# The next pair's h behind xw_lo and the gravity exponentials, not among the t tiles

## The chip, the cores and the metric

The kernel runs on one core of a Trainium2 chip. The metric is the device time of one execution in microseconds; the kernel before was run three times. A separate execution was taken by the hardware profiler. The core's engines are TensorE (PE in the rows: matmul; PEld: its weight loads), VectorE (DVE), ScalarE (ACT), GpSimd (POOL) and SyncE (SP), whose queue issues all the transfers of the main loop.

## The reference

Two graph layers, each followed by a residual add and a layer norm, over x of shape (32, 256, 512). `adj` has shape (256, 256), and the same matrix is the weight of the first layer and the mask of the second.

```python
# layer 1
q = einsum('c,bcn->bn', wq, x); k = einsum('c,bcn->bn', wk, x)
scores = leaky(q[:, None, :] + k[:, :, None])
att = softmax(scores, -1)
out = relu(adj @ (x @ att^T) + bm)
x = layernorm(x + out)                      # this is h, called so below
# layer 2
z_l, z_g, v = h @ W_lang^T, h @ W_grav^T, h @ W_V^T
A_l = relu(cosine(z_l, z_l)) * not_eye
A_g = exp(-|z_g - z_g'|^2 / (2 sigma^2)) * not_eye
K = w_l * rownorm(A_l * adj) + (1 - w_l) * rownorm(A_g * adj)
x = layernorm(h + (K @ v) @ W_O^T)
```

## The kernel before

The 32 batches are done as 16 pairs. Each engine has its own instruction stream, written out by hand, and the streams meet in semaphores; there is no planner. A pipeline of steps p = -2 to 15 works on three pairs at once: in step p the second layer of pair p, the attention and the norm that gives h of pair q = p + 1 (the flag `l0`, true up to p = 14), and the first product of pair r = p + 2 (`new`, up to p = 13). A step in the middle takes some 61 us, and the rows below are mostly of one such step, from 480 to 541 us.

Fp32 accuracy is had from fp16 products of parts: each value is split in a hi part (a cast on ScalarE) and a lo part (value minus hi, on VectorE or GpSimd), and a product is three matmuls, hi by hi, lo by hi, hi by lo. In the profile these are L254, L255 and L256 for every product.

The order of a main step on TensorE is: z products of pair p (L254 to L256 with `ul`, `ug`), attention products of pair q, transposes of the aggregate, the four t products (`t_product`: k = 0, 1 language, k = 2, 3 gravity; two batches each), three xw products of pair r, the adding of transposes (`add_transposed`, L446) and the rows of norms (L261 with `r_l`), the other xw products in between, three v products, the transposes of K (`turn_k`, L478: four for each batch, which wait for `k_done`), `k_rows`, the last v product and the o products.

What the other engines do around the change, in the order of the streams:

- VectorE: `sq_tile` (L1054), `sq_bound` (L1062), `h_tile` (L968: h = (y - mean) * rstd, a tensor_scalar from SBUF to SBUF, 512 columns), `t_lo_tile` (L1069), `neg_g_tile` (L1077), `xw_lo_tile` (L909, L910), `masked_rows`, `a_l_tiles` (L1110), `a_g_tile` (L1093), `q_tops`, then `degrees` (L1117 to L1129, seven instructions on four columns, each waiting for the one before; the last makes `s_l`), `v_lo_tile(0)` (L1048), and `k_tiles` (L1138: K = a_g * s_g + a_l, four instructions of 256 columns, with both tensors in SBUF). Behind these, `kt_lo`, `t_rows`, and the residual adds (L1153).
- ScalarE: `t_hi_tile` (L666, L671), `h_hi_tile` (L700: the cast of an h tile to fp16, into a part of the buffer `att_hi`), `xw_hi_tile` (L616), `exp_tile` (L677), `v_hi_tile` (L683), `k_scale` (L689: a_l times s_l, which waits for `sl_done` and releases the four `k_tiles` one by one).
- GpSimd: `r_l` (L1317), and then `h_lo_tile` (L1274: h minus h_hi, four instructions of 512 columns), each waiting for its h_hi and all of them for the last `t_lo` (`t_lo_done`, 4 p + 4). Elsewhere in the step att_lo (L1291), x_lo (L1297) and two of the four adds of y and x_res (L1305; VectorE does the other two, L946).
- SyncE's queue, in order: `turn_h` (a DMA transpose of h_hi, L215, when all four h_hi are done, and one of h_lo, L218), then the copy of x to `x_res` and the load of the next x. The z products of the next step wait for both transposes (`ht_hi_landed`, `ht_lo_landed`).

In the trace h_hi and h_lo bear the names att_hi and att_lo, v_hi and v_lo the names z_hi and z_lo, the transposed K the names t_hi and t_lo.

Of the kernel before, what the change touches and what calls it, by code (L numbers as in the profile page):

```python
# [51 lines left out]
def build(nc, x, adj, adjT, wqk, bm, wl, wg, wv, woT, gate, sigma, out):  # L52
# [10 lines left out]
    with ExitStack() as ctx:  # L63
# [98 lines left out]
        def h_of(pair):  # L162

            return h2[:, pair % 2]
# [381 lines left out]
        def _(act):  # L546
# [66 lines left out]
            def xw_hi_tile(p, k):  # L613
                r = p + 2
                act.wait_ge(s["wx_mm"], 8 * r + k + 1)
                act.activation(xw_hi[:, k // NC, k % NC, 0:O], wx_bank(p, k)[:, 0:O], ACT.Copy)\  # L616
                   .then_inc(s["xw_hi_done"], 1)
# [30 lines left out]
            def step(p, l0, new):  # L648
                if p < 0:
                    return early(p)  # L650
                q, r = p + 1, p + 2
# [5 lines left out]
                def t_hi_tile(k):  # L657
                    act.wait_ge(s["t_mm"], 4 * p + k + 1)
                    if k < 2:
                        source = halves[4 + k]  # L660
                    else:

                        j = k - 2
                        act.wait_ge(s["neg_g_done"], 2 * p + j + 1)
                        for c in range(OC):
                            last = act.activation(a_g[:, j, c, :], halves[4 + k][:, c, :], ACT.Identity,  # L666
                                                  bias=neg_g[:, 2 * j + c:2 * j + c + 1])
                        last.then_inc(s["shift_done"], 1)
                        act.wait_ge(s["shift_done"], 2 * p + j + 1)
                        source = a_g[:, j]  # L670
                    act.activation(t_hi[:, k], source, ACT.Copy, scale=2.0 ** -6).then_inc(s["t_hi_done"], 1)  # L671

                def exp_tile(j):
                    act.wait_ge(s["s_mm"], 4 * p + 3 + j)
                    act.wait_ge(s["neg_gs_done"], 2 * p + j + 1)
                    for c in range(OC):
                        last = act.activation(halves[6 + j][:, c, :], halves[6 + j][:, c, :], ACT.Exp,  # L677
                                              bias=neg_gs[:, 2 * j + c:2 * j + c + 1], scale=c_grav[:, 0:1])
                    last.then_inc(s["exp_done"], 1)

                def v_hi_tile(k):
                    act.wait_ge(s["v_mm"], 4 * p + k + 1)
                    act.activation(v_hi[:, k, :], bank[v_bank[k]][:], ACT.Copy).then_inc(s["v_hi_done"], 1)  # L683
# [14 lines left out]
                def h_hi_tile(k):  # L698
                    act.wait_ge(s["h_done"], 4 * q + k + 1)
                    act.activation(h_hi[:, k, :], h_of(q)[:, k, :], ACT.Copy).then_inc(s["h_hi_done"], 1)  # L700
# [22 lines left out]
                        z_hi_tile(g)  # L723
                t_hi_tile(0)
                t_hi_tile(1)
                if l0:
                    h_hi_tile(0)
                    h_hi_tile(1)
                t_hi_tile(2)
                if l0:  # L730
                    h_hi_tile(2)
                    h_hi_tile(3)
                t_hi_tile(3)
                if new:
                    for k in range(3):
# [7 lines left out]
                if new:  # L743
                    for k in range(6, 8):
                        xw_hi_tile(p, k)
                exp_tile(1)
                if new:
                    v_hi_tile(0)
                k_scale()
# [17 lines left out]
        def _(dve):  # L767
# [123 lines left out]
            def o_norm(pair, j):  # L891
                if j == 0:
                    dve.wait_ge(s["o_rstd_done"], pair + 1)
                    dve.wait_ge(s["o_mv_done"], pair + 1)
                for k in (2 * j, 2 * j + 1):
                    last = dve.tensor_scalar(o[:, k, :], o[:, k, :], o_mv[:, k, 0:1], o_rstd[:, k:k + 1],  # L896
                                             ALU.subtract, ALU.mult)
                last.then_inc(s["normed"], 1)

            def den(q, k):  # L900
                dve.wait_ge(s["ot_mm"], 8 * q + k + 1)
                wait(dve, s["agg_done"], 8 * (q - 1) + k + 1)
                dve.reciprocal(den_inv[:, k:k + 1], bank[k % 4][:, O:O + 1])\  # L903
                   .then_inc(s["den_done"], 1)
# [8 lines left out]
            def q_tops(r):  # L913
                dve.wait_ge(s["xw_lo_done"], 8 * r + 8)
                dve.tensor_reduce(q_part[:], q_cols, AX.X, ALU.max).then_inc(s["q_part_done"], 1)
# [17 lines left out]
            def att_tile(q, g):  # L933

                j, n = g // NC, g % NC
                dve.wait_ge(s["vb_done"], 8 * q + g + 1)
                wait(dve, s["att_lo_done"], 8 * q + g - 1)
                dve.scalar_tensor_tensor(out=att[:, g % 2, :], in0=a_row[:, j, :], scalar=u_col[:, j, n:n + 1],  # L938
                                         in1=vb_of(q, g), op0=ALU.mult, op1=ALU.max)\
                   .then_inc(s["att_done"], 1)  # L940
# [23 lines left out]
            def h_tile(q, k):  # L964
                if k == 0:
                    dve.wait_ge(s["y_rstd_done"], q + 1)
                    dve.wait_ge(s["y_mv_done"], q + 1)
                dve.tensor_scalar(h_of(q)[:, k, :], y[:, k, :], y_mv[:, k, 0:1], y_rstd[:, k:k + 1],  # L968
                                  ALU.subtract, ALU.mult).then_inc(s["h_done"], 1)
# [66 lines left out]
            def step(p, l0, new):  # L1036
                if p < 0:
                    return early(p)
                q, r = p + 1, p + 2

                def z_lo_tile(g):
                    dve.wait_ge(s["z_hi_done"], 8 * p + g + 1)
                    dve.tensor_tensor(z_lo[:, g, :], bank[g % 4][:], z_hi[:, g, :], ALU.subtract)\  # L1043
                       .then_inc(s["z_lo_done"], 1)
# [44 lines left out]
                def a_g_tile(j):  # L1089
                    dve.wait_ge(s["exp_done"], 2 * p + j + 1)  # L1090
                    for c in range(OC):
                        k = 2 * j + c
                        last = dve.scalar_tensor_tensor(out=a_g[:, j, c, :], in0=halves[6 + j][:, c, :], scalar=1.0,  # L1093
                                                        in1=mask[:, c, :], op0=ALU.min, op1=ALU.mult,
                                                        accum_out=deg_g[:, k:k + 1])
                    last.then_inc(s["ag_done"], 1)
# [60 lines left out]
                def o_stats():  # L1157
                    if p > 0:
                        for k in range(4):
                            o_stat_tile(p - 1, k)  # L1160
                        o_mean(p - 1)

                def o_norms():
                    if p > 0:
                        o_norm(p - 1, 0)
                        o_norm(p - 1, 1)

                if l0:
                    for g in range(8):
                        att_tile(q, g)  # L1170
                        for i, after in enumerate((0, 1, 3, 4, 5, 6, 7)):
                            if g == after:
                                z_lo_tile(i)
                    z_lo_tile(7)
                    den(q, 0)
                    o_stats()
                    for k in range(1, 6):
                        den(q, k)
                    if p > 0:
                        o_norm(p - 1, 0)  # L1180
                    den(q, 6)
                    if p > 0:
                        o_norm(p - 1, 1)
                    den(q, 7)
                    for k in (0, 2):
                        y_add_tile(q, k)
                        y_stat_tile(q, k)
                    y_stat_tile(q, 1)
                    y_stat_tile(q, 3)
                    y_mean(q)  # L1190
                    sq_tile(0)
                    t_lo_tile(0)
                    sq_tile(1)
                    sq_bound()
                    h_tile(q, 0)
                    h_tile(q, 1)
                    t_lo_tile(1)
                    neg_g_tile(0)
                    h_tile(q, 2)
                    h_tile(q, 3)  # L1200
                else:
                    for g in range(8):
                        z_lo_tile(g)
                    o_stats()
                    sq_tile(0)
                    o_norms()
                    t_lo_tile(0)
                    neg_g_tile(0)
                    sq_tile(1)
                    sq_bound()  # L1210
                    t_lo_tile(1)
# [18 lines left out]
                if new:  # L1230
                    xw_lo_tile(p, 6)
                    xw_lo_tile(p, 7)
                    q_tops(r)
                a_g_tile(1)
                degrees()
                v_lo_tile(0)
# [122 lines left out]
```

## Time and profile before

| what | us |
| --- | --- |
| median of three runs | 1048.47 (1047.57 to 1049.12) |
| the profiled execution's own time | 1045.15 |
| its span, first to last instruction | 1043.4 |
| TensorE busy | 1014.2 |
| VectorE busy | 792.3 |
| ScalarE busy | 654.6 |
| GpSimd busy | 385.6 |

Mean granted clock of TensorE: 0.996 of full speed. Busy times are sums over stages that have different limits, and matmuls are pipelined, so they say which engine is full and not what a stage waits for.

### The profile page before, as it was taken

The numbers are of one execution on the slowest core, as the hardware profiler recorded it, in microseconds if no ns is written. First come the engines' busy times: TensorE is split into PE (matmuls) and PEld (weight loads), VectorE is DVE, ScalarE is ACT, GpSimd is POOL, SyncE is SP. The second block draws the span as 40 slices with busy tenths as digits, with TensorE's granted clock in tenths as the row PEclk, the third lists the DMA queues.
The fourth block names the chain that finished last, engine by engine and source line by source line (L and its number), as shares of the span: only waits on it lengthen the run. The fifth ranks groups of instructions, "written<-read, shape, count | busy, mean of one in ns | idle before, by whom it ended". The sixth has DMA issues, their size and how long they took to land.

```text
span 1043.4 us, 19673 instructions
## 1 busy us (share of the span) xinstructions
PE 1014.2 (97%) x7189; PEld 695.5 (67%) x7189; DVE 792.3 (76%) x2318; ACT 654.6 (63%) x1267; POOL 385.6 (37%) x340
## 2 busy tenths in 40 slices
PE   7888999999999999999999999999999999999995
PEld 4465848577584857758485775848577584857662
DVE  5775776878787687878768787876878787787756
ACT  2658576665857666585766658576665857666432
POOL 0335334262533426253242625324262532424200
PEclk9999999999999999999999999999999999999998
DMA  7020221314022141402214140221414022131211
GB/s 271 32 82 1 32 91 52 112 41 107 16 75 88 48 116 41 114 10 72 91 47 117 41 113 10 71 92 46 118 41 106 18 69 94 44 79 41 41 41 41
DMA packets 85233, 72.05 MB, mean 69 GB/s; under 512 B 64144, under 2 KB 64656, under 8 KB 83088
## 3 DMA queue, kind: packets, MB, share of 16 engines
q1 hardware_dynamic: 85136, 70.79, 23.4%
q8 instruction: 57, 0.93, 0.4%
q14 instruction: 40, 0.33, 0.1%
HBM read 21.50 MB, written 16.78 MB: 37 GB/s over the span
## 4 chain that ended last, share of the span: by engine, by line
PE 84%; issue 5%; DVE 1%; ACT 1%; POOL 1%; POOLq 0%; DVEq 0%; ACTq 0%
PE bank L254 25%; PE bank L255 25%; PE bank L256 25%; PE bank L338 3%; PE bank L446 2%; PE bank L261 2%; PE bank L478 1%; POOL att_lo L1274 0%; DVE o L896 0%; ACT bank L578 0%; DVE t_lo L1069 0%; ACT t_hi L671 0%; ACT a_g L666 0%; ACT z_hi L655 0%; POOLq L63 0%
## 5 line engine op out<-in xcount | busy, mean ns | idle before, releaser
L1291 POOL TENSOR_TENSOR att_lo<-att,att_hi 128x512 f16<-128x512 f32 x128 | 148.2, 1158 | 337.4 <-ACT att_hi L584 337.4
L254 PE MATMUL bank<-xw_hi,att_hi 128*128 128x257 f16 x512 | 140.4, 274 | 1.2 <-DVE wvo_lo L858 1.0
L255 PE MATMUL bank<-ht_lo,z_hi 128*128 128x256 f16 x512 | 139.6, 273 | 0.0
L254 PE MATMUL bank<-ht_hi,z_hi 128*128 128x256 f16 x512 | 139.6, 273 | 0.0
L256 PE MATMUL bank<-ht_hi,z_lo 128*128 128x256 f16 x512 | 139.6, 273 | 0.0
L256 PE MATMUL bank<-xw_hi,att_lo 128*128 128x257 f16 x512 | 139.5, 272 | 0.0
L255 PE MATMUL bank<-xw_lo,att_hi 128*128 128x257 f16 x512 | 139.1, 272 | 0.0
L1043 DVE TENSOR_TENSOR z_lo<-bank,z_hi 128x512 f16<-128x512 f32 x128 | 88.2, 689 | 48.1 <-ACT z_hi L655 48.1
L603 ACT ACTIVATE agg_t<-bank,den_inv 128x256 f32<-128x256 f32 x128 | 58.4, 472 | 79.3 <-DVE den_inv L903 78.9
L1274 POOL TENSOR_TENSOR att_lo<-h,att_hi 128x512 f16<-128x512 f32 x60 | 67.6, 1159 | 102.3 <-DVE t_lo L1069 102.3
L683 ACT ACTIVATE z_hi<-bank 128x512 f16<-128x512 f32 x64 | 37.6, 591 | 95.6 <-PE bank L256 95.6
L254 PE MATMUL bank<-wvo_hi,ht_hi 128*128 128x512 f16 x256 | 97.0, 379 | 0.0
L255 PE MATMUL bank<-wvo_lo,ht_hi 128*128 128x512 f16 x256 | 97.0, 379 | 0.0
L256 PE MATMUL bank<-wvo_hi,ht_lo 128*128 128x512 f16 x256 | 97.0, 379 | 0.0
L938 DVE SCALAR_TENSOR_TENSOR att<-a_row,u_col,bank 128x512 f32<-128x512 f32 x120 | 88.7, 739 | 9.8 <-POOL att_lo L1291 7.2
L584 ACT ACTIVATE att_hi<-att 128x512 f16<-128x512 f32 x128 | 80.2, 626 | 23.0 <-DVE att L938 23.0
L655 ACT ACTIVATE z_hi<-bank 128x512 f16<-128x512 f32 x128 | 75.0, 586 | 22.5 <-PE bank L256 22.5
L578 ACT ACTIVATE bank<-b_row,v_col 128x512 f32<-128x512 f32 x120 | 80.7, 680 | 1.2
L1305 POOL TENSOR_TENSOR y<-y,x_res 128x512 f32<-128x512 f32 x32 | 47.0, 1468 | 87.8 <-ACT y L610 87.7
L254 PE MATMUL bank<-wm_hi,x_hi 128*128 128x258 f16 x256 | 70.3, 275 | 4.1 <-DVE x_lo L981 2.5
L256 PE MATMUL bank<-wm_hi,x_lo 128*128 128x258 f16 x256 | 69.8, 273 | 0.0
L255 PE MATMUL bank<-wm_lo,x_hi 128*128 128x258 f16 x256 | 69.8, 273 | 0.0
(177 smaller groups left out, 2629.3 us busy)
## 6 DMA issues: line engine op xcount, KB each, us to landing
x_in<-in_x SPq DMA_DIRECT2D x16, 1024.0 KB, 5.5
x_res<-x_in SPq DMA_DIRECT2D x16, 1024.0 KB, 5.1
out_y<-o SPq DMA_DIRECT2D x32, 512.0 KB, 2.8
agg_t<-in_wl SPq DMA_DIRECT2D x4, 256.0 KB, 3.5
y<-in_wg SPq DMA_DIRECT2D x1, 1024.0 KB, 9.3
o<-in_wv SPq DMA_DIRECT2D x1, 1024.0 KB, 11.5
h<-in_woT SPq DMA_DIRECT2D x1, 1024.0 KB, 13.6
att<-in_adjT SPq DMA_DIRECT2D x1, 256.0 KB, 4.0
```

Source lines behind the costliest of these rows:

```text
L254: pe.matmul(dst, ah, bh, start=(i == 0 and first), stop=False, skip_group_check=skip)
L255: pe.matmul(dst, ah, bl, start=False, stop=False, skip_group_check=skip)
L256: last = pe.matmul(dst, al, bh, start=False, stop=(i == n - 1), skip_group_check=skip)
L578: act.activation(vb_of(q, g), b_row[:, j, :], ACT.Copy, scale=v_col[:, j, n:n + 1])\
L584: act.activation(att_hi[:, g // NC, g % NC, :], att[:, g % 2, :], ACT.Copy)\
L603: act.activation(agg_t[:, k // NC, k % NC, :], bank[k % 4][:, 0:O], ACT.Copy, scale=den_inv[:, k:k + 1]).then_inc(s["agg_done"], 1)
L655: act.activation(z_hi[:, g, :], bank[g % 4][:], ACT.Copy).then_inc(s["z_hi_done"], 1)
L938: dve.scalar_tensor_tensor(out=att[:, g % 2, :], in0=a_row[:, j, :], scalar=u_col[:, j, n:n + 1], in1=vb_of(q, g), op0=ALU.mult, op1=ALU.max)\
L1043: dve.tensor_tensor(z_lo[:, g, :], bank[g % 4][:], z_hi[:, g, :], ALU.subtract)\
L1274: pool.tensor_tensor(h_lo[:, k, :], h_of(q)[:, k, :], h_hi[:, k, :], ALU.subtract)\
L1291: pool.tensor_tensor(att_lo[:, n[0], n[1], :], att[:, g % 2, :], att_hi[:, n[0], n[1], :], ALU.subtract).then_inc(s["att_lo_done"], 1)
L1305: pool.tensor_tensor(y[:, k, :], y[:, k, :], x_res[:, k // 2, k % 2, :], ALU.add)\
```

## The change

The four h tiles of the next pair are computed on VectorE behind the last two `xw_lo` tiles and `q_tops`, in front of `a_g_tile(1)`, and no longer two and two between the t_lo tiles. Their casts h_hi on ScalarE stand behind `exp_tile(1)`, in front of `v_hi_tile(0)` and `k_scale`, and no longer around `t_hi_tile(2)`. In step 14, which has no pair r, the h tiles stand directly behind `a_g_tile(0)`, and the casts in front of `k_scale`. GpSimd's and SyncE's streams are not touched.

```diff
@@ scalar, step @@
                 t_hi_tile(0)
                 t_hi_tile(1)
-                if l0:
-                    h_hi_tile(0)
-                    h_hi_tile(1)
                 t_hi_tile(2)
-                if l0:
-                    h_hi_tile(2)
-                    h_hi_tile(3)
                 t_hi_tile(3)
...
                 exp_tile(1)
+                if l0:
+                    for k in range(4):
+                        h_hi_tile(k)
                 if new:
                     v_hi_tile(0)
                 k_scale()
@@ vector, step @@
                     t_lo_tile(0)
                     sq_tile(1)
                     sq_bound()
-                    h_tile(q, 0)
-                    h_tile(q, 1)
                     t_lo_tile(1)
                     neg_g_tile(0)
-                    h_tile(q, 2)
-                    h_tile(q, 3)
...
                     xw_lo_tile(p, 6)
                     xw_lo_tile(p, 7)
                     q_tops(r)
+                if l0:
+                    for k in range(4):
+                        h_tile(q, k)
                 a_g_tile(1)
                 degrees()
                 v_lo_tile(0)
```

## Rows read from the trace of the kernel before

**Rows 1.** The page, busy us (share of the span), instructions.

```profile
PE 1014.2 (97%) x7189; PEld 695.5 (67%) x7189; DVE 792.3 (76%) x2318; ACT 654.6 (63%) x1267; POOL 385.6 (37%) x340
```

**Rows 2.** Busy times in a stretch: engines, granted clock, DMA share, GB/s.

```profile
480.00:541.00 61.00, 61.00 (x445) 42.31 (x443) 47.71 (x142) 40.54 (x78) 24.55 (x21) 1.00 0.24 70
```

**Rows 3.** Waits of TensorE: for whom, us in total, times, longest.

```profile
PE bank L254 <- DVE z_lo L1043: 5.1, 3, 2.6
```

**Rows 4.** Timeline of VectorE in the middle step: start, us, instruction.

```profile
480.28 1.00 DVE L968 TENSOR_SCALAR h<-y,y_mv,y_rstd 128x512 f32<-128x512 f32 x2
...
484.21 0.29 DVE L1077 SCALAR_TENSOR_TENSOR vb<-bank,ident 128x128 f32<-128x128 f32 x1 [0.99 <-PE bank L256]
...
494.00 0.41 DVE L1093 SCALAR_TENSOR_TENSOR a_g<-bank,mask 128x256 f32<-128x256 f32 x1
...
495.36 0.22 DVE L1129 SCALAR_TENSOR_TENSOR s_l<-deg_l,c_wl,r_l 128x4 f32<-128x4 f32 x1
...
496.23 1.67 DVE L1138 SCALAR_TENSOR_TENSOR a_l<-a_g,s_g,a_l 128x256 f32<-128x256 f32 x4
```

**Rows 5.** Timeline of ScalarE in the middle step.

```profile
480.86 1.15 ACT L700 ACTIVATE att_hi<-h 128x512 f16<-128x512 f32 x2 [1.29 <-DVE h L968]
...
494.33 0.60 ACT L683 ACTIVATE z_hi<-bank 128x512 f16<-128x512 f32 x1 [1.59 <-PE bank L256]
```

**Rows 6.** Timeline of TensorE in the middle step.

```profile
499.31 1.04 PE L478 MATMUL bank<-ident,a_l 128*128 128x128 f32 x8
```

**Rows 7.** Timelines of VectorE, TensorE and GpSimd in step 14.

```profile
978.66 0.39 DVE L1117 TENSOR_TENSOR deg_l<-deg_l,r_l 128x4 f32<-128x4 f32 x1
...
980.39 1.67 DVE L1138 SCALAR_TENSOR_TENSOR a_l<-a_g,s_g,a_l 128x256 f32<-128x256 f32 x4
...
982.61 0.38 PE L254 MATMUL bank<-wvo_hi,ht_hi 128*128 128x512 f16 x1
...
974.53 4.50 POOL L1274 TENSOR_TENSOR att_lo<-h,att_hi 128x512 f16<-128x512 f32 x4 [5.43 <-DVE t_lo L1069]
```

**Rows 8.** Timeline of GpSimd in the middle step.

```profile
488.58 4.51 POOL L1274 TENSOR_TENSOR att_lo<-h,att_hi 128x512 f16<-128x512 f32 x4 [6.89 <-DVE t_lo L1069]
```

**Rows 9.** att tiles: start-up timelines, and the line's forms (ns min/median/max).

```profile
37.87 2.29 POOL L1291 TENSOR_TENSOR att_lo<-att,att_hi 128x512 f16<-128x512 f32 x2 [1.38 <-ACT att_hi L584]
...
39.14 1.57 DVE L938 SCALAR_TENSOR_TENSOR att<-a_row,u_col,vb 128x512 f32<-128x512 f32 x1 [1.34 <-POOL att_lo L1291]
...
L938 DVE SCALAR_TENSOR_TENSOR att<-a_row,u_col,bank x120: 735/739/749, 84.1 to 947.6; 128x512 f32<-128x512 f32 x120
L938 DVE SCALAR_TENSOR_TENSOR att<-a_row,u_col,vb x8: 740/746/1567, 30.6 to 45.5; 128x512 f32<-128x512 f32 x8
```

**Rows 10.** The adds of y and x_res on both engines, ns min/median/max.

```profile
L946 DVE TENSOR_TENSOR y<-y,x_res x32: 691/928/1193, 64.4 to 962.1; 128x512 f32<-128x512 f32 x32
...
L1305 POOL TENSOR_TENSOR y<-y,x_res x32: 1267/1468/1674, 65.1 to 962.7; 128x512 f32<-128x512 f32 x32
```

**Rows 11.** The lines of r_l and of the degree product.

```profile
L1317 POOL TENSOR_TENSOR r_l<-sq_lc,exponent x16: 1006/1232/1234, 114.7 to 1012.8; 128x4 f32<-128x4 f32 x16
...
L1117 DVE TENSOR_TENSOR deg_l<-deg_l,r_l x16: 156/156/390, 128.9 to 1021.0; 128x4 f32<-128x4 f32 x16
```

**Rows 12.** Busy times in stretches of the start-up, columns as in rows 2.

```profile
33.50:36.50 3.00, 0.62 (x2) 0.00 (x0) 2.33 (x8) 2.38 (x6) 1.15 (x1) 1.00 0.00 0
...
37.40:40.80 3.40, 3.40 (x8) 2.08 (x7) 2.06 (x3) 2.20 (x5) 2.29 (x2) 0.50 0.00 0
83.00:86.00 3.00, 0.43 (x3) 0.03 (x2) 1.52 (x3) 2.92 (x7) 0.14 (x1) 1.00 0.00 0
```

**Rows 13.** SP's and TensorE's timelines, and transfers (us to landing).

```profile
493.12 1.93 SPq L218 DMA_TRANSPOSE ht_lo<-att_lo  x1
...
509.04 0.38 PE L254 MATMUL bank<-ht_hi,ul_hi 128*128 128x512 f16 x1
...
ht_lo<-att_lo SPq DMA_TRANSPOSE x15, 4.4
```

## The prediction

> **What bounds the kernel now.** I read the page first. TensorE is busy for 97% of the span [rows 1]. Then the stretches: over 61 us in the middle TensorE is busy for all 61.00 us at full clock, while VectorE has 13 us to spare, ScalarE 20 and GpSimd 36 [rows 2]. TensorE's own waits name z_lo three times, the longest 2.6 us, one of them at 83 us, in the first main step [rows 3, 12]. After some 90 us, until the last product, I find no start-to-start gap on TensorE over 0.45 us. So the reader is to see this: for 14 of the 15 steps that prepare a next pair, TensorE is the bound and waits for nothing. Work that other engines do is free as long as it stays inside its slack, and nothing that they save can come back in the time. The question is only which slack this change uses up.
>
> The step of 480 to 541 us stands for the others; its time is 60.9 us.
>
> **The change part by part.**
>
> *What is removed.* Four h tiles leave the place among t_lo: two pairs of 1.00 us each, at a pitch of 0.46 us (0.54 + 0.46), 1.84 us in all [rows 4]. Behind the second pair VectorE waits 0.99 us for TensorE's next t product, and ScalarE's t_hi of that product needs what VectorE then makes of it, so all behind it comes when it came before. Of the first pair, t_lo of tile 1 comes 0.9 us earlier, but TensorE asks for it only behind the last t product and three xw products, and is busy throughout [rows 2]. Gain: nothing. On ScalarE four casts leave, a pair in 1.15 us, the first of it 0.61 [rows 5]. Nothing again.
>
> *What h now stands in front of.* Behind the last xw_lo, from 494.00, VectorE runs a_g of tile 1, the degrees, s_l, and, after ScalarE's scaling, the four K tiles, which TensorE transposes. This is one chain: s_l ends at 495.58, K tiles run from 496.23 to 497.90 [rows 4]. TensorE starts the eight transposes at 499.31, at a pitch of 0.11, so the second half of them at 499.75 [rows 6]. In the last such step the K tiles end at 982.06, and the product behind the transposes starts at 982.61, so their second half at 982.61 - 0.44 = 982.17: the hand-over takes 0.11 us [rows 7]. Slack of the chain: 499.75 - 497.90 - 0.11 = 1.74 us. The four h tiles push it by 1.84 us. By displacement alone each of 14 steps loses 0.1 us: the cover is all but spent before anything else is counted.
>
> *h_hi and h_lo.* ScalarE has been idle since 492.74 (1.59 us before v_hi) [rows 5], so h_hi of tile 0 starts when h is there: h 494.00 to 494.54, cast 494.62 to 495.23. GpSimd's h_lo waits for h_hi alone now, since the last t_lo is long done; it starts some 0.15 us after, at 495.38. Before, the four h_lo ran from 488.58 to 493.09, all of them over VectorE work that reads PSUM [rows 8]. Now four h_lo of 1.16 us at a pitch of 1.12 us lie from 495.38 on, over h tile 3, the degrees and the K tiles, and these read two operands from SBUF.
>
> *What such an overlap costs.* Four places show it. In the start-up, GpSimd's att_lo runs from 37.87 for 2.29 us, to 40.16; an att tile whose operands all lie in SBUF starts at 39.14 and takes 1.57 us, where its kind has a median of 0.746: it ends 0.54 us after GpSimd does, as if it had only then begun [rows 9]. The y adds on VectorE, two SBUF operands of 512 columns, take 0.69 us at the least, where GpSimd is idle, and 1.19 at the most, beside GpSimd's y tiles [rows 10]. The tiny degree product of four columns takes up to 0.390 us where the median is 0.156, and that is the one of the last such step, where it ends with the last h_lo (979.05 and 979.03) [rows 7, 11]. And r_l on GpSimd has a median of 1.232 us, with two h tiles (tensor_scalars from SBUF to SBUF) beside it from 480.28 to 481.28, and a least of 1.006, that of the last step, which has no h tiles [rows 4, 11]: a tensor_scalar on SBUF holds GpSimd up as well. Where all but one input is in PSUM, nothing is seen: a hundred and twenty att tiles lie between 735 and 749 ns, whether att_lo runs or not [rows 9]. So VectorE's two-SBUF-operand work waits until the running GpSimd instruction ends, however short it is itself.
>
> *The sum of it.* At the y adds the waiting VectorE instruction goes in between GpSimd's two, which follow each other directly: the first of those takes 1.27 us and the second 1.67, the 0.4 to 0.5 more being what the add holds [rows 10]. I take that for the rule: they alternate. From 495.4 on VectorE's contending instructions are h tile 3, the degree product, the two clamps, s_g, s_l and four K tiles, each a dependent small step, so nearly each meets a fresh h_lo, and VectorE is free only when the fourth has ended. That is 495.38 + 4.51 (as the four take now) = 499.89, and 0.5 us later where h tile 3 holds GpSimd back: about 500.5. By then the degrees stand at the second or third of their clamps; 0.4 us remain to the end of s_l, 500.9. From the end of s_l to the second K release it takes 497.90 - 495.58 = 2.32 us: 503.2, plus 0.11: TensorE goes on at 503.3 instead of 499.75, **3.6 us** late. TensorE has nothing else queued ahead of these transposes, and is in order, so all of it is lost. Times 14: 50.4 us.
>
> *Bounds of this term.* Below: no exclusion at all, 0.1 us a step. Between: if the four-column tensor_scalars don't contend (no row shows them beside GpSimd), only the degree product, s_l and the K tiles do; then s_l ends near 498.4, the K tiles alternate with the last two h_lo and end near 502.1, 2.5 us a step. Above: h tile 3 loses the place and the back-to-back h_lo let nobody in: they end at 499.97, then h (0.5), a_g and degrees (1.6), 502.0, plus 2.32: 4.7 us a step. I take 3.6, since the y adds show alternation and r_l under the h tiles shows that a tensor_scalar contends.
>
> On this last point the Trainium skill has a rule (SBUF — State Buffer, Who interferes with whom): a VectorE instruction with two SBUF inputs, and also a tensor_scalar in its two-port mode, and a GpSimd instruction that reads SBUF shut each other out for the whole of one instruction. By it the small clamps wait too and the step loses 3.6 us; by the rows of two-operand instructions alone it would be 2.5 us, and the total some 17 us less with the last step. The trace agrees where it has both (1.57 us for 0.746), and no row has four columns of tensor_scalar beside GpSimd.
>
> *The last such step.* It has no xw work, and the second half of the transposes starts right behind the K tiles, at 982.17 for 982.06 [rows 7]. With no slack the whole delay, 503.2 - 497.9 = 5.3 us, is lost. Once: 5.3 us.
>
> *The clock.* Twice before the steady part TensorE stands still for nearly 3 us. At 33.5 the next stretch is granted 0.50 for 3.4 us, that is 1.2 GHz instead of 2.4, after 0.62 us of work in 3.00; the stall at 83.0, with 0.43 in 3.00, came and went at full clock [rows 12]. One fall in two. A stall of 3.6 us per step is of that kind. A fall costs half of 3.4, 1.7 us. I count 6 in the 15, somewhat under one in two since there is dense work on both sides: 10.2 us (bounds: none, and all 15, 25.5).
>
> *What is behind it, hidden.* SP's queue: the hi transpose can go at 496.9, the lo transpose at 500.5 instead of 493.12. Its landing takes 4.4 us: 504.9, and the products of the next pair start at 509.04 + 3.6 = 512.6 [rows 13]. 7.7 us remain. The x_res copy and the x_in load behind them in the queue slip by the same 7 us; their readers (x_hi, the y adds) stand in the next step behind all eight z tiles, more than 7 us further on. v_hi on ScalarE behind h_hi slips from 494.33 to 496.8, and its v_lo stands just in front of the K tiles, whose turn comes at 501.5. Residuals of pair p read h of pair p, the other buffer. All free.
>
> Sum: 50.4 + 5.3 + 10.2 = 65.9 us on the profiled span of 1043.4, so 1109.3; that execution took 1045.15 (1.75 around the span), and the median of the runs shown is 3.3 above it. **1048.5 + 65.9 = 1114 us.**
>
> **The rivals.** (1) *The displacement alone.* If h_lo and the degrees don't get into each other's way, 14 x 0.1 + 1.84 + 0 = 3.2 us: 1051.7. For it speaks that busy shares leave room; against it the four places above. (2) *Not slower.* The same, with the four h tiles costing 1.74 us or less, the slack: then 14 steps lose nothing and the last loses under 1.84 us, 1050.3 or less, within 0.2% (2.1 us, about what a measurement tells). It decides at 1.74 us of total delay of s_l. Against: the pitch of 0.46 us leaves 1.84. Nothing makes it faster: TensorE has no gap to close but the 0.3 us of the last step. (3) *Partial exclusion.* The small steps slip through between h_lo's, and only one or two of them and the K tiles wait: 1 to 2.5 us a step, with little clock loss, 1065 to 1085. For it: VectorE, once waiting, goes first. (4) *No alternation and a cold clock.* 14 x 4.7 + 6.4 in the last step + 15 falls of 1.7: 98 us, 1146. For it: GpSimd's four follow at a pitch shorter than their length, which two y adds don't.
>
> **How the numbers follow.** Forecast with alternation (2.5 to 4.4 us a step, up to 10 falls): 0.65, that is 1086 to 1134. Rival 3: 0.16. Rival 4: 0.06. Rival 1: 0.06. Rival 2: 0.05. An unforeseen gain: 0.02. Range: 1066 leaves out rivals 1, 2 and the gain (0.13), 1134 leaves out 0.06. Slower: 0.65 + 0.16 + 0.06 + 0.06 = 0.93; same 0.05; faster 0.02.
>
> **What would show it.** In the changed profile: h_lo beginning some 0.15 us behind the first h_hi and lying over the degrees; degree instructions, four columns wide, that take up to 1.1 us; r_l back at 1.0 us; TensorE waiting 3 to 4 us for VectorE's K tiles in front of the transposes in every step, 5 in the last; the granted clock below 1 in several stretches behind such waits. It is wrong if the degree instructions keep 0.16 us beside h_lo, if h_lo begins after the K tiles, or if the alternation gives VectorE most of the turns, when the wait is 1 to 2 us.

## The result and the profile after

| | us |
| --- | --- |
| median before, beside this one | 1048.02 (1045.34 to 1049.12, 4 runs) |
| median after | 1108.13 (1107.30 to 1110.47, 4 runs) |
| ratio | 1.0581, 95% interval 1.0554 to 1.0608 |
| profiled span after | 1107.2, against 1043.4 |

The change costs 60 us, 5.8%. The same instructions run; of the span's 63.8 us more, TensorE's busy time takes 26.6 (1040.8 for 1014.2), and the rest is time in which it stands still. The page's first part and the waits of TensorE after the change:

```profile
PE 1040.8 (94%) x7189; PEld 713.1 (64%) x7189; DVE 837.1 (76%) x2318; ACT 656.8 (59%) x1267; POOL 384.8 (35%) x340
```

```profile
PE bank L478 <- DVE a_l L1135: 36.5, 15, 3.9
PE bank L254 <- DVE z_lo L1040: 5.1, 3, 2.6
```

The second wait is the one of [rows 3]; the first is new, stands in all 15 steps that prepare a next pair, and names the K tiles. (VectorE's lines have moved up by three: h is L965, the degrees L1114 to L1126, the K tiles L1135. The h_lo line of GpSimd is L1270.) Here is VectorE in the middle step. TensorE, before its stall, is 26.80 us behind the step of [rows 4 to 8], so that 520.81 stands for 494.01:

```profile
520.81 2.80 DVE L965 TENSOR_SCALAR h<-y,y_mv,y_rstd 128x512 f32<-128x512 f32 x4
...
524.21 0.43 DVE L1114 TENSOR_TENSOR deg_l<-deg_l,r_l 128x4 f32<-128x4 f32 x1
524.56 0.16 DVE L1116 TENSOR_SCALAR deg_g<-deg_g 128x4 f32<-128x4 f32 x1
524.67 1.09 DVE L1118 TENSOR_SCALAR deg_l<-deg_l 128x4 f32<-128x4 f32 x1
525.67 0.16 DVE L1120 RECIPROCAL deg_g<-deg_g 128x4 f32<-128x4 f32 x1
525.79 0.18 DVE L1122 RECIPROCAL deg_l<-deg_l 128x4 f32<-128x4 f32 x1
525.89 0.98 DVE L1124 TENSOR_SCALAR s_g<-deg_g,c_wg 128x4 f32<-128x4 f32 x1
526.78 0.21 DVE L1126 SCALAR_TENSOR_TENSOR s_l<-deg_l,c_wl,r_l 128x4 f32<-128x4 f32 x1
...
527.65 1.67 DVE L1135 SCALAR_TENSOR_TENSOR a_l<-a_g,s_g,a_l 128x256 f32<-128x256 f32 x4
```

GpSimd's four h_lo in the same step, one by one:

```profile
522.16 1.16 POOL L1270 TENSOR_TENSOR att_lo<-h,att_hi 128x512 f16<-128x512 f32 x1 [13.89 <-ACT att_hi L700]
...
523.27 1.34 POOL L1270 TENSOR_TENSOR att_lo<-h,att_hi 128x512 f16<-128x512 f32 x1
...
524.58 1.15 POOL L1270 TENSOR_TENSOR att_lo<-h,att_hi 128x512 f16<-128x512 f32 x1
...
525.70 1.14 POOL L1270 TENSOR_TENSOR att_lo<-h,att_hi 128x512 f16<-128x512 f32 x1
```

Read the two side by side. The first h_lo ends at 523.32, and the fourth h tile ends at 523.60 instead of 522.7: alone it would have taken 0.54 us, not 2.80 - 3 x 0.46 = 1.42. The second h_lo ends at 524.61, the degree product at 524.64. The third ends at 525.73, the clamp of deg_l at 525.76. The fourth ends at 526.84, s_g at 526.87. Each of these small VectorE instructions ends 0.03 us behind the h_lo that it meets, though it has four columns of its own; the three that don't meet one (the clamp of deg_g right behind a wait, s_l, the K tiles) keep their lengths. What it makes of the degree lines over all steps, and of r_l on GpSimd, which has no h tile beside it any more (ns min/median/max; compare [rows 11]):

```profile
L1114 DVE TENSOR_TENSOR deg_l<-deg_l,r_l x16: 159/428/432, 134.6 to 1084.8; 128x4 f32<-128x4 f32 x16
L1118 DVE TENSOR_SCALAR deg_l<-deg_l x16: 166/1086/1090, 135.1 to 1085.0; 128x4 f32<-128x4 f32 x16
L1124 DVE TENSOR_SCALAR s_g<-deg_g,c_wg x16: 230/981/983, 136.3 to 1085.3; 128x4 f32<-128x4 f32 x16
L1313 POOL TENSOR_TENSOR r_l<-sq_lc,exponent x16: 1006/1006/1007, 117.7 to 1076.6; 128x4 f32<-128x4 f32 x16
```

The least of each degree line is that of step 15, which has no h. TensorE at the transposes, in three successive steps and in step 14, and in stretches around the second of them (columns as in [rows 2]):

```profile
528.59 1.45 PE L478 MATMUL bank<-ident,a_l 128*128 128x128 f32 x8 [2.31 <-DVE a_l L1135]
...
592.40 1.91 PE L478 MATMUL bank<-ident,a_l 128*128 128x128 f32 x8 [2.31 <-DVE a_l L1135]
...
657.83 1.91 PE L478 MATMUL bank<-ident,a_l 128*128 128x128 f32 x8 [2.31 <-DVE a_l L1135]
...
1043.89 1.97 PE L478 MATMUL bank<-ident,a_l 128*128 128x128 f32 x8 [3.94 <-DVE a_l L1135]
```

```profile
590.00:593.00 3.00, 0.69 (x5) 0.42 (x4) 2.94 (x7) 2.15 (x6) 0.66 (x1) 1.00 1.11 203
...
593.10:596.50 3.40, 3.30 (x15) 3.13 (x16) 3.34 (x7) 1.49 (x3) 0.00 (x0) 0.50 1.11 342
```

From 528.59 to 592.40 it is 63.81 us, against 60.93 before (499.31 to 560.24): 2.88 us a step, made of 2.47 in front of the first transposes and 0.4 among the eight, most of it in front of their second half, which waits for the last K tiles. From 592.40 to 657.83 it is 65.43: here the clock fell to 1.2 GHz for 3.41 us, from 593.1 on, as in the second stretch.

### The profile page after: what moved, and what is told of

Read it like the earlier page. It is cut to its first block, busy times and chain, and to the rows that moved or that the text cites. A ratio compares the mean times of both kernels' runs of the same rounds, so it can differ in the third digit from the quotient of the medians.

```text
span 1107.2 us, 19673 instructions
## 1 busy us (share of the span) xinstructions
PE 1040.8 (94%) x7189; PEld 713.1 (64%) x7189; DVE 837.1 (76%) x2318; ACT 656.8 (59%) x1267; POOL 384.8 (35%) x340
## 4 chain that ended last, share of the span: by engine, by line
PE 62%; DVE 20%; issue 6%; ACT 3%; POOL 1%; DVEq 0%; POOLq 0%; ACTq 0%
PE bank L254 18%; PE bank L256 18%; PE bank L255 18%; DVE h L965 4%; DVE xw_lo L907 3%; PE bank L338 3%; PE bank L261 2%; DVE a_l L1107 2%; PE bank L478 2%; DVE a_g L1090 2%; DVE a_l L1135 2%; DVE a_l L1098 1%; DVE deg_l L1118 1%; ACT a_g L666 1%; DVE s_g L1124 1%
## 5 line engine op out<-in xcount | busy, mean ns | idle before, releaser
L1270 POOL TENSOR_TENSOR att_lo<-h,att_hi 128x512 f16<-128x512 f32 x60 | 70.2, 1200 | 205.1 <-ACT att_hi L700 205.1
```

What stands on the lines that cost most here:

```text
L1270: pool.tensor_tensor(h_lo[:, k, :], h_of(q)[:, k, :], h_hi[:, k, :], ALU.subtract)\
```

## The experiments

All were run beside the kernel before, with their ratio to it. The step is the distance from one step's first transpose of K to the next one's, in the middle of the trace, where the clock is full.

| kernel | h moved | h_lo | time, us | ratio (95%) | step, us |
| --- | --- | --- | --- | --- | --- |
| before | none | early | 1047.45 | | 60.93 |
| the change | 4 | over the degrees | 1108.13 | 1.0581 (1.0554 to 1.0608) | 63.81 |
| change, h_lo held | 4 | behind K | 1051.65 | 1.0038 (1.0025 to 1.0052) | 61.04 |
| two tiles, h_lo held | 2 | behind K | 1048.96 | 1.0017 (1.0007 to 1.0027) | 60.93 |
| casts alone | 0 | over the degrees | 1061.51 | 1.0134 (1.0113 to 1.0155) | 61.70 |
| change, TensorE filled | 4 | over the degrees | 1092.87 | 1.0436 (1.0414 to 1.0457) | 63.82 |
| two tiles, h_lo free | 2 | 2 early, 2 over the degrees | 1060.45 | 1.0119 (1.0103 to 1.0134) | 61.69 |
| before, h_lo held | none | behind K | 1049.48 | 1.0009 (1.0000 to 1.0019) | 60.92 |

The change had 1048.02 beside it, the first four experiments 1047.45, the last two 1047.71.

**The change with h_lo held.** One line more on GpSimd, nothing else:

```diff
                         pool.wait_ge(s["t_lo_done"], 4 * p + 4)
+                        pool.wait_ge(s["k_done"], 2 * p + 2)
```

> The change with one wait more: GpSimd's h_lo also waits until both halves of K are done. The h tiles and their casts stand where the change puts them. Theory (exclusion): the degrees go back to 0.16 us an instruction, and only the displacement of 1.84 us over a slack of 1.74 is left: 0.1 us in each of 14 steps and about 1.8 in the last, some 1051 us, full clock in the steady part. The last h_lo ends near 504.4 in the middle step's time and its transpose lands near 508.8, just ahead of the z products at 509.1; if that is too late, some tenths of a us a step come on top. Rival (the four h tiles ahead of the degrees are the cost, wherever h_lo is): 1090 us or more.

Measured: 1051.65. The degree instructions are back to their lengths, on VectorE; GpSimd's h_lo start once K is done; and TensorE's transposes wait 0.1 us a step:

```profile
496.88 0.16 DVE L1114 TENSOR_TENSOR deg_l<-deg_l,r_l 128x4 f32<-128x4 f32 x1
497.00 0.17 DVE L1116 TENSOR_SCALAR deg_g<-deg_g 128x4 f32<-128x4 f32 x1
497.08 0.17 DVE L1118 TENSOR_SCALAR deg_l<-deg_l 128x4 f32<-128x4 f32 x1
...
498.42 1.67 DVE L1135 SCALAR_TENSOR_TENSOR a_l<-a_g,s_g,a_l 128x256 f32<-128x256 f32 x4
```

```profile
500.23 4.50 POOL L1270 TENSOR_TENSOR att_lo<-h,att_hi 128x512 f16<-128x512 f32 x4 [18.41 <-DVE a_l L1135]
...
504.76 1.93 SPq L218 DMA_TRANSPOSE ht_lo<-att_lo  x1
...
499.66 1.15 PE L478 MATMUL bank<-ident,a_l 128*128 128x128 f32 x8
...
560.70 1.15 PE L478 MATMUL bank<-ident,a_l 128*128 128x128 f32 x8
```

So the four h tiles stand where the change puts them, and 56 of the 60 us are gone. What is left in the steps is the displacement alone: 61.04 - 60.93 = 0.11 us a step. The z products (TensorE from 509.51 in this trace) don't wait, though the transpose of h_lo was issued at 504.76. Of the 4.2 us that remain in all, 14 x 0.11 = 1.5 are these, 1.4 come from the transposes of K in step 14, and 0.8 from the added wait itself, as the control below shows.

**Two tiles, h_lo held.** VectorE and, likewise, ScalarE move tiles 2 and 3 only; the wait of the last experiment stays.

```diff
                     t_lo_tile(1)
                     neg_g_tile(0)
-                    h_tile(q, 2)
-                    h_tile(q, 3)
...
                     q_tops(r)
+                if l0:
+                    h_tile(q, 2)
+                    h_tile(q, 3)
                 a_g_tile(1)
```

> Only h tiles 2 and 3 and their casts are moved, tiles 0 and 1 stay among the t tiles, and h_lo waits for both halves of K as in the run beside this one. Displacement 0.92 us, under the slack of 1.74. Theory: nothing in 14 steps, 0.9 us in the last: 1049, not to be told from before. Rival (VectorE's order costs by itself, without a threshold): half of what four tiles cost.

Measured: 1048.96, and 60.93 us a step to the hundredth, so no step but the last pays for 0.92 us of displacement. The transposes' row is that of [rows 6] again:

```profile
500.53 1.04 PE L478 MATMUL bank<-ident,a_l 128*128 128x128 f32 x8
...
561.46 1.04 PE L478 MATMUL bank<-ident,a_l 128*128 128x128 f32 x8
```

With 0.11 us a step for 1.84, this brackets the threshold between 0.92 and 1.84 us; if each us beyond it costs one, it lies where the slack of 1.74 was read. In step 14 the first transposes start 0.43 us late and the second half 0.35, where before it was 0 and 0.26.

**ScalarE's part alone.** The four casts behind `exp_tile(1)`, the h tiles where they were before.

```diff
                 t_hi_tile(1)
-                if l0:
-                    h_hi_tile(0)
-                    h_hi_tile(1)
                 t_hi_tile(2)
-                if l0:
-                    h_hi_tile(2)
-                    h_hi_tile(3)
...
                 exp_tile(1)
+                if l0:
+                    for k in range(4):
+                        h_hi_tile(k)
```

> Only ScalarE's part: the h tiles stay among the t tiles on VectorE, the four casts stand behind the gravity exponentials. No displacement on VectorE; h_lo runs from about 493.4 to 498.0 in the middle step's time, over the degrees and into the K tiles. Theory: the end of s_l comes 2 to 3 us late, 1.74 of it inside the slack: 0.3 to 1.2 us a step and 2.5 in the last, 1055 to 1068. Rival (displacement by h is the cost): 1048, unchanged.

Measured: 1061.51, 61.70 us a step. VectorE isn't displaced at all here, and its degree lines show three waits:

```profile
502.91 1.02 DVE L1114 TENSOR_TENSOR deg_l<-deg_l,r_l 128x4 f32<-128x4 f32 x1
503.86 0.16 DVE L1116 TENSOR_SCALAR deg_g<-deg_g 128x4 f32<-128x4 f32 x1
503.97 1.09 DVE L1118 TENSOR_SCALAR deg_l<-deg_l 128x4 f32<-128x4 f32 x1
...
505.19 0.98 DVE L1124 TENSOR_SCALAR s_g<-deg_g,c_wg 128x4 f32<-128x4 f32 x1
```

```profile
501.64 4.50 POOL L1271 TENSOR_TENSOR att_lo<-h,att_hi 128x512 f16<-128x512 f32 x4 [11.73 <-ACT att_hi L700]
```

The excess over the lengths without GpSimd is 0.86 + 0.92 + 0.75 = 2.5 us; less the slack, 1.74, it leaves 0.8 us, and the step is 0.77 longer. In step 14, which has no slack, the first transposes start 3.3 us late. So moving four casts on ScalarE, an engine that is idle a third of the time, costs 14 us through two engines whose streams are not edited.

**The change with TensorE filled.** Ten products that nothing reads, in the stall:

```diff
                 v_product(2)
+                if l0:
+                    pe.wait_ge(s["ag_done"], 2 * p + 1)
+                    for i in range(10):
+                        pe.matmul(bank[6][:], ident16[:], ul_hi[:, 0, :], start=True, stop=True)
                 turn_k(0)
```

> The change, with ten needless fp16 products of 512 columns (some 2.2 us) on TensorE in front of the transposes of K in the 15 steps with a next pair, into a PSUM bank that is free there; nothing reads them. The stall stays as long for what follows, but TensorE isn't idle in it. Theory: the twelve falls of the clock in the steady part (3.41 us each at half rate) go away, 12 x 1.7 = 20 us: 1088, mean clock 0.99. Rival (the falls fall on time that TensorE would lose anyway, or don't come from the stalls): 1108 as the change.

Measured: 1092.87, so 15 us less than the change, for more work (and 17.4 us less in the profiled spans). In TensorE's timeline the filling stands in front of the transposes, which start no later for it:

```profile
516.38 2.32 PE L534 MATMUL bank<-ul_hi,ident 128*128 128x512 f16 x10
518.87 1.45 PE L478 MATMUL bank<-ident,a_l 128*128 128x128 f32 x8 [0.17 <-DVE a_l L1139]
...
582.69 1.45 PE L478 MATMUL bank<-ident,a_l 128*128 128x128 f32 x8 [0.17 <-DVE a_l L1139]
```

The step is 63.82 us, the change's own where the clock didn't fall, and every step of this run is such a one: between 500 and 1026 us the granted clock is 1.00, where the change has 0.98. The one fall left in the steps is in step 14, behind the longest stall. The falls are the stalls' doing, and they cost on top of them. Less came back than the 20 us that I had worked out: 15.3 us for eleven falls is 1.4 each and not 1.7, for which see below.

**Two tiles, h_lo free.** The two-tile kernel without the wait.

> Only h tiles 2 and 3 and their casts are moved, as in the earlier run with two tiles, but GpSimd's h_lo isn't held back. h_lo of tiles 0 and 1 runs early as before; the other two run from about 495.4 to 497.6 in the middle step's time, over the degrees. Theory: the degree product waits until 496.5 and the next clamp but one until 497.6, s_l ends near 498.1, 2.5 us late for a slack of 1.74: 0.8 us a step and some 2.3 in the last, no fall of the clock in the steady part, 1058 to 1064 us. Rival (the displacement of 0.92 us decides, and it is under the slack): 1049 as the held run.

Measured: 1060.45, against 1048.96 for the same with h_lo held. VectorE:

```profile
501.55 0.86 DVE L1117 TENSOR_TENSOR deg_l<-deg_l,r_l 128x4 f32<-128x4 f32 x1
502.34 0.15 DVE L1119 TENSOR_SCALAR deg_g<-deg_g 128x4 f32<-128x4 f32 x1
502.45 1.08 DVE L1121 TENSOR_SCALAR deg_l<-deg_l 128x4 f32<-128x4 f32 x1
```

Two h_lo, two waits: 0.70 + 0.91 us, with 0.92 of displacement 2.5 us, less 1.74 of slack 0.8; the step is 0.76 longer. It adds up as the casts alone do, from another mix of the two terms. The rival, by which the displacement decides, would have had it at 1049. In step 14 the first transposes start 1.98 us late, and a fall of the clock follows at 996.8 us; the casts alone, 3.3 us late there, have none.

**Before, with h_lo held.** The control for the wait itself.

> The kernel before, with GpSimd's h_lo held until both halves of K are done, so that its transpose is issued near 504.4 and lands near 508.8, before the z products at 509.04. Theory: no change, 1047 to 1049 us: what the held runs cost is theirs and not the wait's. Rival (the late transpose or the later h_lo costs some tenths a step): 1050 to 1055.

Measured: 1049.48, ratio 1.0009 with an interval from 1.0000 to 1.0019, and 60.92 us a step. The wait costs nothing in the steps up to 13. It does cost once, in front of the z products of step 15, where these come 9.0 us behind the first transposes of K (981.42 and 990.38 us before) and not 9.7 as in the middle (499.31 and 509.04). The transpose of h_lo, issued at 979.06 before, goes at 988.84 here and lands at 993.17; TensorE starts the first z product 0.98 us behind the product before it, where 0.22 is usual:

```profile
988.84 1.92 SPq L218 DMA_TRANSPOSE ht_lo<-att_lo  x1
```

```profile
993.26 0.38 PE L254 MATMUL bank<-ht_hi,ul_hi 128*128 128x512 f16 x1 [0.60 <-issue]
```

The profile names no releaser for this wait, but the landing is 0.09 us ahead of it, and both other held kernels have the same 0.98 us there (at 994.23 with four tiles, where the landing is at 994.14, and at 992.90 with two). So 0.76 us of what the held kernels lose is the wait's, and the rest theirs; it agrees in size with the ratio of 1.0009. A single profiled span can't tell so little: the start-up alone puts the transposes of step 2 at 255.43 us before and at 257.70 here.

## Why the prediction was right

By its own steps:

- **What is removed gives nothing.** Right. The one thing in which the old place had a price, r_l at 1.232 us, fell to 1.006 and nobody waited for it.
- **The slack, 1.74 us, and the displacement, 1.84.** Right, and shown: 0.11 us a step for four tiles, none for two. (My hand-over of 0.11 us has two parts. In step 14 of the kernel before the second half starts at 982.12, 0.06 behind the K tiles, and the other 0.05 is the pitch of its first transpose, 0.16 for 0.11.)
- **Exclusion between h_lo and VectorE's SBUF work.** Right, and shown four ways: by the lengths of the degree instructions in the change, by holding h_lo (1108 to 1052), by the casts alone (no displacement, 14 us), by freeing h_lo of the two-tile kernel (1049 to 1060). That four-column tensor_scalars wait too was the part that no row of before had; the clamp at 1.09 us and s_g at 0.98 show it. Here the Trainium skill's rule (SBUF — State Buffer, Who interferes with whom) and the trace agree, in that the wait lasts to the end of the running GpSimd instruction. Whether the K tiles wait too, as I had it, the middle steps don't show: h_lo has ended before them in each of these kernels, or starts behind them.
- **Its size, 3.6 us a step: measured 2.88, the term that was mis-sized.** The fourth h_lo ends at 526.84, in the old step's time 500.04, where I had 500.5. But I had the K chain resume with 0.4 us of degrees to go and 500.9 for s_l; it ends at 526.99, or 500.19. The waits are 0.88 (h), 0.27, 0.92 and 0.75 us, 2.8 in all, not one of 1.1 for nearly each instruction: the clamp of deg_g comes directly behind a wait and starts at 524.56, just ahead of the third h_lo at 524.58, and the two reciprocals don't contend, so that s_g, the last but one, is what waits for the fourth. 1.84 + 2.8 - 1.74 = 2.9.
- **Step 14, 5.3 us:** 4.10 in front of the first transposes and 0.47 in front of the second half, less the 0.26 of before, is 4.3. The forecast is 1.0 too high here, for the same reason in the main.
- **The clock: 6 falls, 10.2 us; there were 12.** Mis-sized in number, and the other way. Of the 15 stalls 12 are followed by a stretch at 0.50 of 3.41 us. I had taken one start-up fall in two stalls as the rate, and then gone under it. A single fall costs less than the 1.7 us that I had: from the first transposes of step 0 (139.02 us) to those of step 13 (982.67), 13 steps take 51.4 us more than before, 37.4 of them in stalls of 2.88, and the other 14.0 are ten falls, 1.4 each. That part of a slow stretch falls on time in which TensorE would have waited for K anyway is my explanation, not tested. Without the stalls, 63.8 - 14 x 2.88 - 4.3 = 19.2 us are left on the span. Of these 3.0 lie in the start-up, ahead of the first stall, where this trace has one fall more than that of before and where the control above is 2.3 us later too: they are not the change's. That leaves 16.2 for the twelve falls.
- **What is behind, hidden.** Right for the change: the wait for K is the only one of TensorE's waits that is new. With h_lo held, where the lo transpose is issued at 504.76, the steps up to 13 still hide it, and only step 15 waits, 0.76 us.

The terms were off in opposite directions: -11.1 us for the stalls (2.88 for 3.6, 4.3 for 5.3), +6.0 for the falls and +3.0 of start-up that no term had. That the sum of 65.9 us on the span stands beside 63.8 measured is in part luck: with the stalls as they measured and the clock as forecast it would have been 54.8. The other 4 us to the median lie between the profiled executions and the medians: I had put the median 3.3 us over the profiled execution's time, as before, and after the change it lies 0.8 under it (1108.13 for 1108.90). The clocks on record fit that: executions of the kernel before with a mean granted clock of 0.996 took 1045.25 and 1045.66 us, those with 0.989 or 0.990 took 1048.2 to 1050.6, and the profiled one was of the first kind.

**The rivals.** Displacement alone is what the held kernel measures, 1051.65 for 1051.7, and it isn't the change. No exclusion, or a partial one, is refuted by the rows. The back-to-back lock (4.7 us) is too: h tile 3 went in between the first and the second h_lo, whose length grew to 1.34 us.

No version here beats the kernel before, and its rows leave this route nothing to win: TensorE waits for nothing in 14 steps, and for 0.26 us in the last one with a next pair.

## What to carry to other kernels

Before moving work on an engine that has time to spare, find the next hand-over to the bound engine behind its new place and read the slack of that chain; here 1.74 us, and 1.84 were put in. Then ask what the move triggers on a third engine and what that overlaps: 93% of the loss came from GpSimd work that nobody edited, laid by the move over the last h tile and the degree steps on the critical chain, where four short VectorE instructions had to wait for it. Where a move is wanted anyway, one added wait that keeps the two apart takes the loss from 60 us to 4.

## What the runs showed of the hardware

- A VectorE instruction of four columns, with two SBUF operands or a tensor_scalar on SBUF, ends 0.03 us after the GpSimd instruction that it meets: 0.43 to 1.09 us instead of 0.16 to 0.23. Reciprocals of four columns (0.16 to 0.18) and the a_g tiles, with one operand in PSUM (0.41 at 523.52 and 523.86, beside the second h_lo), don't. With two or more GpSimd instructions back to back VectorE gets its turn at each boundary (four times in a step of the change), and a second instruction slips in if it follows at once (the clamp of deg_g, 0.16).
- Stalls of 2.9 us in TensorE, 61 to 65 us apart (4.3 us in step 14), were followed by a clock of 0.50 for 3.41 us in 12 of 15 cases, at 1.4 us each in the steps. The 0.8 us a step of the casts-alone kernel never were. The length alone doesn't decide: in step 14 a delay of 1.98 us (two tiles, h_lo free) was followed by a fall, and one of 3.3 us (casts alone) wasn't. Needless products in the stall removed 11 of the 12 and bought back 15 us, though the transposes started no earlier for it.
